# Other stage sizes and another product schedule in a staged weighted reduction with a matrix product (Trainium2, one core)

## What is computed

```python
# x: (1024, 24, 1024)   W1: (1024, 24)   b1, b2: (1024,)   W2: (1024, 1024), all float32
h = jax.nn.sigmoid(jnp.einsum('bts,st->bs', x, W1) + b1)   # weighted sum over t = 0..23
y = h @ W2.T + b2                                          # contraction over s
```

## Time and profile before

| | us |
|---|---|
| median of three executions | 320.87 |
| profiled execution, its own time | 322.97 |
| its span, first to last instruction | 321.2 |
| PE busy | 269.7 (84%) |
| DVE busy | 261.1 (81%) |
| POOL busy | 166.0 (52%) |
| mean of the granted TensorE clock | 0.963 of full |

### The profile page before, as it was taken

How to read it: one execution, slowest core, us unless ns; L and a number is a source line. 1 busy time by engine, 2 the same in 40 slices (tenths; PEclk the granted TensorE clock), 3 DMA queues, 4 the chain that set the end, 5 groups by cost and what they waited for, 6 DMA issues and landing times.

```text
span 321.2 us, 4852 instructions
## 1 busy us (share of the span) xinstructions
PE 269.7 (84%) x1825; PEld 231.9 (72%) x1825; DVE 261.1 (81%) x392; ACT 45.0 (14%) x79; POOL 166.0 (52%) x63
## 2 busy tenths in 40 slices
PE   0846868648889999999799999949999988599775
PEld 0746767548768888888588888848888967488664
DVE  0717999929999988889998888988888999377956
ACT  1201212002262001000500000040111140000030
POOL 0009687600009999942399750059889419760000
PEclk9969989969999999999999999998999999799999
DMA  7999999999999999999999999999999996996006
GB/s 237 407 388 390 386 385 386 400 386 387 385 386 384 369 386 387 386 387 376 371 312 375 384 384 389 383 375 373 373 372 373 361 348 217 349 294 203 1 0 261
DMA packets 67367, 109.99 MB, mean 342 GB/s; under 512 B 3208, under 2 KB 40080, under 8 KB 67344
## 3 DMA queue, kind: packets, MB, share of 16 engines
q1 hardware_dynamic: 66608, 107.06, 93.7%
q10 hardware_dynamic: 736, 2.63, 2.0%
HBM read 105.48 MB, written 4.19 MB: 341 GB/s over the span
## 4 chain that ended last, share of the span: by engine, by line
PE 60%; DMA 27%; SPq 4%; issue 4%; DVE 4%; DVEq 0%
PE xbank L206 31%; DMA ring<-in_r_x 27%; PE pbank L263 24%; PE xbank L291 3%; DVE acc L315 2%; SPq L175 2%; SPq L169 2%; PE pbank L235 1%; PE pbank L291 1%; DVE w_lo L322 1%; DVE acc L312 0%; DVE y L330 0%; SPq L177 0%; SPq L157 0%; DVE h_lo L348 0%
## 5 line engine op out<-in xcount | busy, mean ns | idle before, releaser
L315 DVE SCALAR_TENSOR_TENSOR acc<-xbank,w,acc 128x512 f32<-128x512 f32 x304 | 215.6, 745 | 45.1 <-PE xbank L206 43.5
L206 PE MATMUL xbank<-ident,ring 128*128 128x128 f32 x1280 | 189.4, 284 | 40.9 <-DMA ring<-in_r_x 39.4
L206 PEld LDWEIGHTS xbank<-ident,ring 128*128 128x128 f32 x1280 | 157.4, 146 | 72.7 <-issue 25.2
L437 POOL TENSOR_TENSOR nat<-nat,w1all 128x2048 f32<-128x2048 f32 (+2 forms) x15 | 55.5, 3703 | 13.7 <-DMA nat<-in_r_x 13.7
L440 POOL TENSOR_TENSOR nsum<-nsum,nat 128x2048 f32<-128x2048 f32 (+2 forms) x15 | 55.5, 3702 | 1.2
L445 POOL TENSOR_TENSOR h_lo<-h,h_hi 128x512 fp32r<-128x512 f32 x14 | 17.5, 1279 | 74.3 <-ACT h_hi L410 74.3
L263 PE MATMUL pbank<-w_hi,h_hi 128*128 128x512 f32 x112 | 49.7, 444 | 0.0
L263 PE MATMUL pbank<-w_lo,h_hi 128*128 128x512 f32 x112 | 48.1, 429 | 0.0
L263 PE MATMUL pbank<-w_hi,h_lo 128*128 128x512 f32 x112 | 41.9, 439 | 0.0
L435 POOL TENSOR_TENSOR nsum<-nat,w1all 128x2048 f32<-128x2048 f32 (+2 forms) x5 | 18.5, 3697 | 22.0 <-ACT w1all L363 22.0
L381 ACT ACTIVATE h<-acc,b1col 128x512 f32<-128x512 f32 (+1 forms) x22 | 11.6, 597 | 107.3 <-DVE acc L315 107.3
(11 more groups left out here) (33 smaller groups left out, 86.9 us busy)
## 6 DMA issues: line engine op xcount, KB each, us to landing
ring<-in_r_x SPq DMA_DIRECT2D x40, 1024.0 KB, 14.3
ring<-in_r_x SPq DMA_DIRECT2D x40, 768.0 KB, 11.8
ring<-in_r_x SPq DMA_DIRECT2D x20, 512.0 KB, 8.2
nat<-in_r_x SPq DMA_DIRECT2D x8, 1024.0 KB, 14.3
nat<-in_r_x SPq DMA_DIRECT2D x8, 768.0 KB, 11.0
y<-in_L_rec_W SPq DMA_DIRECT2D x2, 2048.0 KB, 14.8
out_y<-y ACTq DMA_DIRECT2D x4, 512.0 KB, 6.4
nat<-in_r_x SPq DMA_DIRECT2D x4, 512.0 KB, 8.4
```

Source lines behind the costliest of these rows:

```text
L206: mm = pe.transpose(xbank[u % XBANKS][:, j * P:(j + 1) * P], tile[:, j, :], ident[:, :])
L315: nc.vector.scalar_tensor_tensor(out=acc[:, c, rows], in0=xbank[u % XBANKS][:, rows], scalar=weight, in1=acc[:, c, rows], op0=ALU.mult, op ...
L437: nc.gpsimd.tensor_tensor(slot, slot, row, ALU.mult).then_inc(nat_weighed, 1)
```

## The change

Two edits. The second group's stages get 4, 3 and 1 chunks instead of 3, 3 and 2. In `steps_due`, `lead` becomes the stage's number of chunks (so products begin behind the first slice and one more unit) instead of 10 units, and in the last stage they end at three fifths of the units instead of four fifths. The second edit holds for stage 1 of the first group too.

```diff
@@ STAGES
-    (4, 4, 0, 3, (0, 3, 10, 14), "keep"),
-    (4, 4, 3, 3, (0, 3, 10, 14), "add"),
-    (4, 4, 6, 2, (0, 3, 10, 14), "last"),
+    (4, 4, 0, 4, (0, 3, 10, 14), "keep"),
+    (4, 4, 4, 3, (0, 3, 10, 14), "add"),
+    (4, 4, 7, 1, (0, 3, 10, 14), "last"),
@@ def steps_due(i, v)
             steps = outs[i - 1] * 3 * chunks[i - 1]
-            lead = 10 * JT // tiles[i]
-            span = (len(units[i]) * 4) // 5 - lead
+            lead = chunks[i]
+            span = (len(units[i]) * (3 if i == LAST else 4)) // 5 - lead
             return max(0, min(steps, -(-(v - lead + 1) * steps // span)))
```

## The result

The changed kernel takes 334.9 us (median of four executions, 334.08 to 335.57); the kernel before took 323.02 in the same comparison. The ratio is 1.040 [1.031, 1.049]: **slower by 4%**, where the forecast was 326.8 and the range ended at 331.5. The profiled execution took 335.02 us with a span of 333.2; the mean granted clock fell from 0.963 to 0.944.

What follows compares the result with a forecast made beforehand. It took PE (60%) and transfers (27%) as bounding the kernel in turn. Chain +1.2, slow clock +4.4 in stages 1 to 3 and +0.3 in stage 4 made +5.9 on 320.87: 326.8 us, range 319.5 to 331.5.

Steps and rivals of the forecast that it cites:

- The pauses at four starts: At the starts of stages 1 to 4, PE stands still for h_hi, 3.1 to 4.8 us each.
- The chain of PE at full clock: Stages 1 to 4: PE sets the pace, with first products at 97.87, 162.4, 226.9 and 281.1 us.
- The clock in stages 1 to 4: Half clock behind the new pauses costs 4.4 us in stages 1 to 3 and 0.3 in stage 4.
- The tail: After the last unit: 24 products instead of 48, 1.3 + 5.3 + 3.65 us, with no clock fall priced.
- Nine units are left, as before: DVE's units behind stage 4's last products take 7.2 us, as in the kernel before, to 312.1.
- Stage 4's products: 72 products with 10 units between them and new waits take 23.8 us, to 304.9.
- The four waits: PE's waits within stage 4: 1.2 us for h_lo and 1.7 in all for three banks.
- The level: Whole kernel: the added 5.9 us are counted from the kernel before's median of 320.87, 2.1 below its profiled execution.
- 322.4 + 4.7: Whole span: 322.4 us by the chain at full clock, plus 4.4 and 0.3 for clock falls.
- the clock holds: Rival for the new pauses: the clock does not fall behind them, so +1.2, 322.1 us; chance 0.17.
- Loads end the last stage: Rival for stage 4's last load: decides from 5.1 us to landing; at 7.6 adds 2.5, 329.3 us; chance 0.16.
- Transfers remain the pacemaker: Rival for stages 1 to 3: PE makes up its late starts, stage 3 ends at 272.4, 316.0 us; chance 0.07.

Runs made afterwards that it cites:

- Experiment 8: Changed kernel with idle identity transposes on PE ahead of the four h_hi waits (26, 22, 10, 36) and the tail (34): 327.53 us, 1.016.
- Experiment 9: Kernel before with the last stage's third and fourth special loads at positions 14 and 18 instead of 10 and 14: 319.8 us, 0.989.
- experiment 7: Changed kernel with two accumulators used in turn in the last stage, joined by one addition at its end: 334.88 us, 1.037 of the kernel before.
- experiment 3: Changed kernel with products of stages 1 to 3 beginning behind unit 10, as before the change: 331.31 us, 1.031 of the kernel before.
- experiment 1: Kernel before with the new stage sizes (4, 3, 1) alone and the old steps_due: 339.14 us, 1.056.
- experiment 10: Kernel before with the last stage's special loads at (0, 3, 14, 18) and 30 idle transposes ahead of the tail: 318.49 us, 0.988.
- experiment 2: Kernel before with the new steps_due alone and the old stage sizes (3, 3, 2): 331.22 us, 1.028.
- experiment 5: Changed kernel with 34 idle identity transposes on PE ahead of the tail only: 333.08 us, 1.031 of the kernel before.
- experiment 6: Kernel before with 30 idle identity transposes on PE between its last unit and the tail: 320.34 us, 0.995.

## Why the prediction was wrong

The direction and the mechanism were right, the size was not: +11.9 us against the kernel before, where +5.9 was forecast. Point by point, in us of the span:

- **The pauses at four starts: right.** 3.43, 2.82, 3.48 and 4.28, the second a little below the 3.1 to 4.8 that was worked out, each released by ACT's `h_hi`.
- **The chain of PE at full clock: right.** Experiment 8 starts its stages within 0.6 of the forecast. The loads didn't end stage 3: PE and DVE did.
- **The clock in stages 1 to 4: right in sum.** 4.4 + 0.3 forecast, 4.7 + 0.3 measured. In part that is luck: the three falls cost 1.6, 1.0 and 2.0 us where 1.75 was taken for each, and three falls came where 2.5 were counted. The wait for `h_lo` covers most of stage 4's fall: 1.1 us at full clock, none at half.
- **The tail: the step that failed.** "The sixth, 3.65 us ahead of the tail, left it at full" was one observation, and the forecast put the tail's fall at nothing, while five falls of six were the odds at the other starts. The new wait was 4.13 us, the clock fell behind it, for most of 6.3 us, and that cost 2.6. Experiment 9 shows that not even 3.65 us are safe: the same wait in all but the same kernel brought a fall. Seven traces have no filler ahead of the tail, with waits there from 3.51 to 4.63 us, and the kernel before's is the only one with full clock behind it.
- **"Nine units are left, as before": the second.** In time they are not as before: with one chunk each unit waits for the unit just ahead and adds to the tile that it wrote, and DVE's starts are 0.85 apart instead of 0.66. That is 1.4 us, and experiment 7 shows the cause: with this dependence taken away the same units are over in the 7.2 us of the sum. A row of before with two units on one tile in a row didn't exist; the price was copied from two chunks without a bound.
- **Stage 4's products** took 24.6 at full clock, not 23.8 (0.8). The four waits show as 2.4 us of idle time (1.10 for `h_lo`, then 0.51, 0.28 and 0.51 for banks), where 2.9 was worked out; but by the distance between starts each costs some 0.3 more than its idle time, 3.5 in all. The small rest is in products and units. Stages 1 to 3 ran 0.5 longer than worked out, clock aside, their falls 0.3, and stage 1 began 0.5 later.
- **The level.** The terms above, 2.6 + 1.4 + 0.8 + 0.5 + 0.3 + 0.5, are the 6.1 by which the span, 333.2, passes 322.4 + 4.7. The other 2.1 of the miss come from taking the kernel before at its median of 320.87, below its own profiled execution; in the comparison it took 323.02, close to the 322.97 of that execution.

Of the rivals, "the clock holds" is out by all five falls. "Loads end the last stage" is out too: a load of 256 KB landed in 2.9 us, below the 5.1 from which it would have decided, and PE's one wait of 1.10 for them ended at 315.99, while DVE had units to add without a gap until 318.63. "Transfers remain the pacemaker" needed stage 2's products over by 206; they ended at 214.84. The Trainium skill's formula in "DMA: Bandwidth & Descriptors", section "Anatomy of one DMA", some 2.0 us plus bytes/436e3, given for another issue path, makes 2.6 us for one such load, an estimate; the trace's 2.9 is near it. Its rule against small loads decided nothing here: PE waited for them only once in that stage, and off the path.

So the time went to two things. An order that makes an in-order engine wait, though only for 14 us in all, cost clock behind each wait; and the last stage, made small to shorten the tail, gave back 7.0 of the 19.0 us that its later start had taken. Of these 19.0, 15.3 are there without the early start in stages 1 to 3 too (experiment 3), so most of them belong to the chunk that the sizes move ahead of the last stage. The forecast had 17.7 us for the later start, slow clock included, and 11.8 given back; so it failed mainly in what the last stage gives back, by the tail's clock and the nine units ahead of it.

## What to carry over

Ahead of putting dependent work earlier on an engine that works in order, work out when its input is ready: what the engine can't do in the meantime is lost, and for TensorE the half clock behind the pause can come on top (0.3 to 2.6 us each here). Where such a pause couldn't be avoided, a fitted number of idle transposes kept the clock at no cost that the trace shows; too many of them ended up on the path. A unit price holds only for the same pattern of dependence, and one lucky observation of the clock is no price at all.

## What the runs showed of the hardware

- The same pause of 3.65 us ahead of the tail was followed by full clock in the kernel before and by 0.60 from 304 to 308 in experiment 9. So it is with pauses of 2.70 to 2.72 us for the ring near the start of stage 3: in some 4 us behind them the clock was 0.59 in the kernel before and 0.64 in experiment 9, but full in experiments 1, 3 and 10.
- The fall can come behind the pause, not in it: in experiment 2 the window of the first 1.2 us had a clock of 0.92, the next 4 us 0.60.
- Behind each of the changed kernel's five waits, 2.8 to 4.3 us long, the windows show a clock of 0.51 to 0.60. The Trainium skill says in "TensorE: Matmul & The Clock Gate", section "HAM oscillation — how this bites in real kernels", that waits for data can bring the clock down again and again; the five windows agree.
- With transposes of a 128 x 128 identity, 0.11 us each, in the pauses, the clock stayed at 1.00 through and behind all five in experiment 8, and ahead of the tail in experiments 5, 6 and 10.
- DVE's multiply-and-add over 128 x 512 starts every 0.66 us into changing tiles, and every 0.85 where each waits for the one just ahead and adds to its tile (experiment 7 and the changed kernel).
